# An eleven-block transformer step on one core: in masked attention two of four transposed score tiles get their mask by a ScalarE copy and a GpSimd addition

## The reference, cut to what matters

```
q, k, v = heads(x @ wq + bq), heads(x @ wk + bk), heads(x @ wv + bv)   # 16 heads of depth 16
scores = einsum('bhqd,bhkd->bhqk', q, k) / sqrt(16)
scores = scores + (1.0 - attention_mask * padding_mask) * -1e9          # only in the first attention
attn = softmax(scores); out = einsum('bhqk,bhkd->bhqd', attn, v) @ wo + bo
...
amax = max(abs(x2d), axis=-1); x_scale = maximum(amax, 1e-6) / 127.0
x_q = clip(round(x2d / x_scale), -128, 127)                             # 8-bit layer
```

## Time and profile before

| | before |
|---|---|
| median of 3 runs | 1608.37 us (1607.35 to 1613.48) |
| the profiled execution | 1603.58 us, its span 1601.8 us, mean granted clock 0.899 |
| PE busy in the span | 81% |
| DVE busy | 59% |
| ACT busy | 41% |
| POOL busy | 29% |

### The profile page before, as it was taken

One profiled execution on the slowest core, in us unless ns is written; L12 is line 12 of the kernel. 1 busy time (PEld: TensorE's weight loads), 2 busy tenths in 40 slices (PEclk: granted clock), 3 DMA queues, 4 the chain that ended last, 5 costly groups with the idle time before them and its releaser, 6 DMA issues. The chain is left out here.

```text
span 1601.8 us, 17931 instructions
## 1 busy us (share of the span) xinstructions
PE 1300.8 (81%) x5544; PEld 568.2 (35%) x5545; DVE 948.9 (59%) x2143; ACT 664.1 (41%) x1238; POOL 465.0 (29%) x608
## 2 busy tenths in 40 slices
PE   3588877878788989979969979988898669897970
PEld 1131232322323333523523523532323235564640
DVE  3699989899886655465465466457575132232323
ACT  1155545455455646355345345345555411021220
POOL 4260534422212322163163263234111006100016
PEclk9598989989899999979989979979999779998995
DMA  3833422313433521212212222223321088322214
GB/s 113 278 115 79 132 79 74 126 53 118 141 86 96 173 82 54 92 54 60 74 53 60 73 53 60 73 80 84 101 69 41 33 276 270 122 81 72 82 49 148
DMA packets 134343, 158.53 MB, mean 99 GB/s; under 512 B 15088, under 2 KB 111856, under 8 KB 134000
## 3 DMA queue, kind: packets, MB, share of 16 engines
q1 hardware_dynamic: 115568, 130.19, 26.5%
q10 hardware_dynamic: 15616, 18.88, 3.6%
q0 software_dynamic: 3072, 8.39, 1.6%
HBM read 93.87 MB, written 62.96 MB: 98 GB/s over the span
## 5 line engine op out<-in xcount | busy, mean ns | idle before, releaser
L1027 DVE TENSOR_REDUCE Mx<-bank 128x1 f32<-128x512 f32 x512 | 341.6, 686 | 299.4 <-PE bank L813 295.7
L727 ACT ACTIVATE prob<-bank 128x512 f32<-128x512 f32 x512 | 290.1, 594 | 272.8 <-PE bank L829 271.2
L813 PE MATMUL bank<-KS,QS 96*128 96x512 bf16 x768 | 318.9, 415 | 76.5 <-DVE Mx L1027 43.1
L829 PE MATMUL bank<-QS,KS 99*128 99x512 bf16 x768 | 314.2, 411 | 61.6 <-DVE prob L1038 28.3
L727 ACT ACTIVATE prob<-prob 128x512 f32<-128x512 f32 x256 | 161.0, 629 | 181.6 <-DVE prob L1038 180.0
L842 PE MATMUL bank<-prob,V 128*17 128x512 f32 x1536 | 231.3, 678 | 0.7 <-ACT prob L727 0.7
L813 PEld LDWEIGHTS bank<-KS,QS 96*128 96x128 bf16 x768 | 77.0, 100 | 303.1 <-DVE Mx L1027 116.0
L829 PEld LDWEIGHTS bank<-QS,KS 99*128 99x128 bf16 x768 | 76.4, 100 | 279.4 <-ACT prob L727 130.9
L561 POOL TENSOR_TENSOR rstd<-ve,minus_half 128x4 f32<-128x4 f32 x28 | 28.7, 1025 | 288.7 <-DVE ve L976 288.7
L581 POOL TENSOR_SCALAR MR<-neg 16x128 bf16<-16x128 f32 x48 | 13.8, 288 | 310.0 <-ACT neg L701 310.0
L1038 DVE TENSOR_TENSOR prob<-bank,ff_h 128x512 f32<-128x512 f32 x128 | 87.7, 685 | 17.6 <-PE bank L829 17.2
(11 more groups left out here) (151 smaller groups left out, 1742.1 us busy)
## 6 DMA issues: line engine op xcount, KB each, us to landing
stack_scr<-parts SPq DMA_DIRECT2D x48, 384.0 KB, 2.6
QS<-stack_scr SPq DMA_DIRECT2D x48, 384.0 KB, 4.0
KS<-stack_scr SPq DMA_DIRECT2D x48, 384.0 KB, 4.8
stack_scr<-parts SPq DMA_DIRECT2D x48, 256.0 KB, 2.9
w_gu<-in_gate_up ACTq DMA_DIRECT2D x16, 512.0 KB, 4.7
stack_scr<-parts SPq DMA_DIRECT2D x48, 128.0 KB, 2.7
disp<-zero SPq DMA_DIRECT2D x2, 3072.0 KB, 12.8
xr<-disp SPq DMA_DIRECT2D x48, 128.0 KB, 2.0
```

What stands on the lines that cost most here:

```text
L727: act.activation(prob[:, U % NP_, j, :], src, ACT.Exp, scale=CAST).then_inc(exp_done, 1)
L813: pe.matmul(bankS[i % NS][:, :], QS[0:STACK, v, qt * P:(qt + 1) * P], KS[0:STACK, v, :], start=True, stop=True).then_inc(s_full, 1)
L829: pe.matmul(bankT[e % NT][:, :], KS[0:ROWS, h, kt * P:(kt + 1) * P], QS[0:ROWS, h, :], start=True, stop=True).then_inc(t_full, 1)
L1027: dve.tensor_reduce(dst, b, AX.X, ALU.max).then_inc(s_read, 1)
```

## The change

1. In streams 0 to 3 the transposed tiles with j = 0 and 2 are no longer read by DVE: ACT copies the tile from PSUM to `prob` (`move`), POOL adds the mask in place (`plus_mask`), and ACT takes the exponential (`exponent`). Tiles with j = 1 and 3 stay as they were. The exponential of tile j = 2 stands in the next unit, after the copy of its tile 0; `values` moves from slot 2 to slot 3.
2. The preparation of a mask is an operation of its own, `fill`; it stands directly behind the transfer `mask` except for `fill(0, 1)`, which moves from step 2 to step 5, behind two cuts. `fill(0, 0)` is now DVE's.
3. Prologue: DVE takes the first statistics before its blank fills; the three rows of ones in `KS` come by a transfer in place of a DVE memset; ACT loads its table with a dummy exponential.
4. Layer norms: DVE's addition of epsilon is now POOL's. `affine` and `residual` work in halves of 128x512 in place of 128x1024.
5. Quantisation: the row scale (`xscale`) is worked out by POOL in place of DVE, the reciprocal stands a step later, POOL only does the first of three passes, DVE clamps, and ACT takes the offset away and writes bf16.

```diff
-            put(late, s - 1, ("mask", p, 0))
+            put(late, s - 1, ("mask", p, 0), ("fill", p, 0))
             put(late, s if p == 0 else max(s, first - 6), ("mask", p, 1))
+            put(late, 5 if p == 0 else max(s, first - 6), ("fill", p, 1))
...
-            put(early, e + 2, *halves("apply", p, a), ("affine", p, a))
-            put(late, e + 4, ("turn", p, a), ("res", p, a))
+            put(early, e + 2, *halves("apply", p, a), *halves("affine", p, a))
+            put(late, e + 4, ("turn", p, a), *halves("res", p, a))
...
+                            sp.dma_start(KS[STACK:ROWS, :, :].rearrange("r h (c q) -> r (h c) q", q=P),
+                                         ones_b[0:ROWS - STACK, :].unsqueeze(1)
+                                         .broadcast_to([ROWS - STACK, H * S // P, P])).then_inc(ones_in, 16)
...
+                def step_of(p):
+
+                    pool.wait_ge(amax_ready, p + 1)
+                    pool.tensor_scalar(xscale[p][:, :], amax[:, :], 1e-6, 1.0 / 127.0, ALU.max, ALU.mult)\
+                        .then_inc(xscale_ready, 1)
+
+                def plus_mask(n, u, j):
+
+                    U = n * UNITS + u
+                    if u < QT and j == 0:
+                        pool.wait_ge(mask_ready[1], QT * n + u + 1)
+                    pool.wait_ge(t_moved, moved(U, j))
+                    pool.tensor_tensor(prob[:, U % NP_, j, :], prob[:, U % NP_, j, :],
+                                       mb[n % 2][:, QT + u % QT, :], ALU.add).then_inc(t_added, 1)
...
+                    act.wait_ge(t_masked if j % 2 else t_added, moved(U, j))
+                    act.activation(dst, dst, ACT.Exp, scale=CAST).then_inc(exp_done, 1)
...
+                    if j == 1 and 0 <= u - 1 < (UNITS - 1 if n == B - 1 else UNITS):
+                        exponent(n, u - 1, 2)
                     if 0 <= u < UNITS:
...
+                        if j % 2 == 0:
+                            move(n, u, j)
+                        if j == 3:
+                            exponent(n, u, 0)
+                        if j % 2:
+                            exponent(n, u, j)
...
-                    link(dve.tensor_reduce(amax[:, :], T[p][:, :, :], AX.X, ALU.max, apply_absolute_value=True))
-                    link(dve.tensor_scalar(xscale[p][:, :], amax[:, :], 1e-6, 1.0 / 127.0, ALU.max, ALU.mult))
+                    dve.tensor_reduce(amax[:, :], T[p][:, :, :], AX.X, ALU.max, apply_absolute_value=True)\
+                        .then_inc(amax_ready, 1)
...
-                    if 0 <= u - 1 < UNITS and j == AV_AT:
+                    if 0 <= u - 1 < UNITS and j == (AV_AT if n >= B else HG - 1):
                         values(n, u - 1)
...
-                    if n < B and 0 <= u < UNITS:
+                    if n < B and 0 <= u < UNITS and j % 2:
                         masked(n, u, j)
```

More of the change, by code:

```diff
@@ L82, in batch_order @@
             put(early, s, *halves("apply", p, 0))
-            put(late, s, ("turn", p, 0), ("res", p, 0))
+            put(late, s, ("turn", p, 0), *halves("res", p, 0))
             for i, (m, what) in enumerate(((0, "k"), (0, "q"), (1, "k"), (1, "q"))):
@@ L122, in batch_order @@
                 put(early, e + 20, *halves("apply", p, 4))
-                put(late, e + 20, ("amax", p), ("res", p, 4))
-                put(early, e + 21, ("quant", p))
-                put(late, e + 22, ("i8T", p))
-                put(early, e + 23, ("i8turned", p))
+                put(late, e + 20, ("amax", p), *halves("res", p, 4))
+                put(early, e + 21, ("xrec", p))
+                put(late, e + 21, ("quant", p))
+                put(early, e + 22, ("clamp", p), ("round", p))
+                put(early, e + 23, ("i8T", p))
+                put(early, e + 24, ("i8turned", p))
                 put(late, e + 24, ("i8", p))
@@ L129, in batch_order @@
                 put(early, e + 26, *halves("apply", p, 5))
-                put(late, e + 26, ("turn", p, 5), ("res", p, 5))
+                put(late, e + 26, ("turn", p, 5), *halves("res", p, 5))
         for g in range(NG):
@@ L168, in batch_order, with moved @@
     return order
+def moved(U, j):
+    return 2 * U + j // 2 + 1
 def max_group(u):
@@ L628, in masks, with affine @@
                         link(pool.tensor_scalar(m, m, pm_col[p][:, kt:kt + 1], 1.0, ALU.mult, ALU.add))
-                        pool.tensor_scalar(m, m, NEG, 0.0, ALU.mult, ALU.add).then_inc(mask_ready[p], 1)
-                def affine(p, i):
+                        pool.tensor_scalar(m, m, NEG, 0.0, ALU.mult, ALU.add).then_inc(mask_ready[1], 1)
+                def affine(p, i, half):
                     if (p, i) == (0, 1):
@@ L667, in _ @@
                         quantise(*at)
-                    elif kind == "mask":
+                    elif kind == "fill" and at != [0, 0]:
                         masks(*at)
+                    elif kind == "amax":
+                        step_of(*at)
+                    elif kind == "tiles" and at[0] < B and 0 <= at[1] < UNITS and at[2] % 2 == 0:
+                        plus_mask(*at)
                     elif kind == "affine":
@@ L736, in _, with exponent @@
-                act.wait_ge(consts_dve, 2)
+                def exponent(n, u, j):
+                    U = n * UNITS + u
+                    e, dst = U * HG + j, prob[:, U % NP_, j, :]
+                    if n >= B:
+                        act.wait_ge(t_full, e + 1)
+                        act.activation(dst, bankT[e % NT][:, :], ACT.Exp, scale=CAST).then_inc(exp_done, 1)
+                        return
+                    act.wait_ge(t_masked if j % 2 else t_added, moved(U, j))
+                    act.activation(dst, dst, ACT.Exp, scale=CAST).then_inc(exp_done, 1)
@@ new lines, in move, with out_read @@
+                def move(n, u, j):
+                    U = n * UNITS + u
+                    e = U * HG + j
+                    act.wait_ge(t_full, e + 1)
+                    act.activation(prob[:, U % NP_, j, :], bankT[e % NT][:, :], ACT.Copy).then_inc(t_moved, 1)
+                def out_read(n, u):
+                    g = n * NG + u // QT - 1
+                    act.wait_ge(av_done, n * UNITS + u)
+                    if g >= 2:
+                        act.wait_ge(m_full, JOB[("oT", (g - 2) // NG, (g - 2) % NG)] + 1)
+                    act.activation(oT[:, g % 2, :], bankO[:, :], ACT.Copy).then_inc(o_read, 1)
@@ L737, in _ @@
+                act.wait_ge(consts_pool, 8)
+                act.activation(warm[:, :], ones_b[:, 0:1], ACT.Exp)
+                act.wait_ge(early_in, EARLY)
                 for kind, *at in ORDER:
@@ L745, in _ @@
                         normalise(*at)
+                    elif kind == "round":
+                        p = at[0]
+                        act.wait_ge(clamped, p + 1)
+                        act.activation(xq[p], T[p][:, :, :], ACT.Identity, bias=minus_magic[:, 0:1])\
+                            .then_inc(xq_ready, 1)
                     elif kind in ("turn", "attT"):
@@ L1081, in _ @@
                         statistics(*at)
+                        if at == [0, 0, 1]:
+                            blanks()
+                            dve.wait_ge(early_in, EARLY)
+                    elif kind == "fill" and at == [0, 0]:
+                        first_mask()
+                    elif kind == "xrec":
+                        shares(*at)
+                    elif kind == "clamp":
+                        clamp(*at)
                     elif kind == "apply":
```

172 lines of the change are left out of this document (100 added, 72 removed).

## The result

The changed kernel takes 1636.04 us (median of 4 runs, 1634.73 to 1639.88) beside 1608.56 us of the kernel before on the same chip: a ratio of 1.0169, 95% interval 1.0141 to 1.0196. It is slower by 1.7%; forecast were 1555 us.

The account below looks back on a forecast made before the run. DVE was taken to bound the masked streams (90% busy) and PE those without mask. Prologue 20.7, masked streams 20 (60 less 40) and quantisation 12 off 1603.6 gave 1550.9, put at 1555 us as the execution was 4.8 under median; range 1515 to 1590.

Parts of the forecast that it names:

- Part 1: Prologue: earlier statistics and POOL's split no longer delayed bring the first score tile at 32.7 us, a gain of 20.7 us.
- Part 2: Masked streams: moving 128 of DVE's 256 additions to ACT copies and POOL additions gains 60 us, before mask preparation losses.
- the ceiling is 77 us: Masked streams: most that removing 128 DVE additions at 0.60 us each could gain, checked against stream 4's 77.5 us.
- Part 3: Masked streams: mask preparations on POOL now stand ahead of its tile additions and lose 40 us of the 60.
- the three second masks: Preparations of batches 1 to 3's second masks on POOL delay additions: 5.5, 3 and 3 us lost.
- The first masks: Preparations of batches 1 to 3's first masks on POOL delay tiles: 8, 10 and 10 us lost.
- The others run on for a while: While POOL's addition is late, PE goes on until slot 2 of the next unit, about 3.5 us.
- Part 4: Quantisation: DVE's scale operation, held by POOL's additions up to 4.11 us, moves to POOL; 12 us gained.
- (A): Rival: queues are elastic and the mask preparations cost nothing, 1515 us; chance 0.16 (below 1530).
- (B): Rival: other POOL work between additions also costs; masked streams gain nothing or lose up to 25, 1575 to 1600; chance 0.15.
- (C): Rival: POOL's additions and DVE hold each other up in the masked streams, 1661 us; chance 0.07 including any other loss.
- or another loss: Any loss of the whole kernel by a cause not listed; no size given, shares the chance 0.07 with (C).

Follow-up runs that it names:

- e15_dve_finer: e9_finer with all four transposed tiles of a group masked by DVE as in the kernel before; 1583.01 us, 0.9827 of the kernel before.
- e9_finer: e2_spread with the two halves of each residual and scale-and-shift put a step apart in all layers; 1557.48 us, 0.9693 of the kernel before.
- e3_dve_tiles: Changed kernel with all four transposed tiles masked by DVE again and `values` in slot 2; 1598.67 us, 0.9805 of the kernel before.
- e8_no_tmask: e3_dve_tiles without DVE's mask additions on transposed tiles, exponentials reading PSUM; 1520.43 us, 0.9450 of the kernel before.
- e4_nofill: Changed kernel with earlier mask transfers and the mask preparations of batches 1 to 3 left out; 1600.14 us, 0.9805 of the kernel before.
- e2_spread: Changed kernel with earlier mask transfers and each preparation of batches 1 to 3 spread over four steps; 1597.70 us, 0.9791 of the kernel before.
- e0_after: The changed kernel measured again without edit, on the chip of some follow-up runs; 1660.86 us, 1.0201 of the kernel before.
- e11_scale_dve: Changed kernel with the quantisation's 128x4 scale operation moved back from POOL to DVE; 1640.52 us, 1.0202 of the kernel before.

## Why the prediction was wrong

**Part 1 was right**, 32.1 us for 32.7. The first mask's preparation on DVE ended in time, though it met POOL's residual in the prologue:

```profile
14.52 3.19 POOL L691 TENSOR_TENSOR R<-R,b_row 128x512 f32<-128x512 f32 x2 [5.90 <-DMA b_row<-in_brow]
```

```profile
14.15 0.43 DVE L1091 TENSOR_SCALAR mask<-mask 128x512 f32<-128x512 f32 x1
...
15.21 1.37 DVE L1091 TENSOR_SCALAR mask<-mask 128x512 f32<-128x512 f32 x1
```

The same DVE operation took 0.43 us and then 1.37 beside the residual. By the Trainium skill, "SBUF — State Buffer", section "SBUF: two separate sides", the one of the two engines that starts first has the shared ports for its whole instruction when DVE is in a two-port mode, or reads two inputs from SBUF beside a GpSimd operation that reads it. The trace agrees: this operation took 0.94 us longer, the next one, with two inputs, 1.75 us where the one before had taken 0.69, and POOL's pair 3.19 us where such a pair takes 2.48 at 74.20 us.

**Part 2 failed**, in the step "the ceiling is 77 us ... I take 60 of the 77, by estimate, so 0.94 us of a plain unit's 4.8", that is, 0.94 us in each of 64 units. Measured: 5.5 us with spread preparations (382.3 to 376.8), 14.4 with finer pieces (382.3 to 367.9; 18.5 against e15_dve_finer), 11.7 with POOL's additions out. In e9_finer the 16 units 9 to 12 did give 12.3 us against e3_dve_tiles, 0.77 each; the other 48 gave 2.1 together. The ceiling priced every one of DVE's additions at 0.60 us, from a plain unit, and checked it against the 77 us of stream 4; e8_no_tmask, without any of them, takes 76.7 us in stream 0 but 80.7 to 87.1 in streams 1 to 3, where the layer work of two batches sets the length of some units. All 256 are worth 52.7 us, so 128 could not bring 77. Against the half that is given away stand the copies, 8 to 10 us, and POOL's lateness, 10 to 12 against e4_nofill and 6 to 8 against e2_spread. PE's waits show what came in DVE's place. In the masked streams of e3_dve_tiles PE waited 64.3 us for DVE and 1.7 for ACT and POOL, in e9_finer 31.7 and 31.4. The largest of both (e3_dve_tiles first):

```profile
PE bank L908 <- DVE prob L1136: 26.7, 92, 1.2
PE bank L888 <- DVE Mx L1122: 22.6, 78, 0.9
```

```profile
PE bank L907 <- DVE Mx L1143: 13.4, 43, 0.8
PE bank L929 <- DVE prob L1157: 13.1, 35, 1.2
PE bank L929 <- ACT prob L787: 11.2, 17, 3.4
PE bank L942 <- ACT oT L796: 7.5, 12, 0.8
PE bank L868 <- POOL R L687: 5.9, 3, 2.1
PE bank L868 <- ACT R L766: 5.4, 2, 2.9
```

Half of the waiting for DVE has gone and as much waiting for ACT's copies and results and for layer norm rows (`R`) of ACT and POOL has come. The forecast had taken 17 us off its ceiling for such coupling. Why the first half of the additions brings so much less than the second is not settled beyond that; DVE's remaining additions stand in slots 1 and 3 with a maximum behind each, and no run evened them out.

**Part 3 had the mechanism and was too small**: 40 us taken, 64.0 measured as the difference of e0_after and e2_spread (4.6 before the first values product, 59.4 behind it), of which 39.5 are POOL waiting and 24.5 POOL computing. The terms that were mis-sized are the three second masks, 5.5 us for batch 1 and "I take 3 each" for batches 2 and 3: the two units around each (3 and 4 of streams 0, 1 and 2) were 14.0, 13.9 and 16.1 us longer than the same units before, as in the changed order additions stand right behind the preparation, and the output projection does not cover it. The first masks were near the forecast: 4.6 us ahead of the first values product where 8 were taken, and units 13 to 15 of streams 0 and 1 longer by 11.2 and 11.8 us where 10 each were. "The others run on for a while" gave back 2.6 us in that place and not 3.5: PE stood 9.25 us for an addition that came 11.9 us after the one before it had ended (110.99 less 99.11). And the half clock after each stop was not in the sum: PE's busy time for the same 1343 to 1346 records is 315.7 us in e0_after and 305.5 in e2_spread, 10 of the 59, beside granted clocks of 0.87 and 0.92.

**Part 4 had the size; its cause is at most a part.** -9.8 us where -12 was forecast, and no operation of 4 us. PE's waits for row maxima in streams 4 to 10 fell from 38.6 to 19.3 us, where the forecast had three waits of over 4 us in mind. But the held operation put back cost nothing, and with its collision mostly taken out of the kernel before streams 6 to 9 were 5.6 us shorter, of 13.7 that the change gains there, and the whole kernel no faster (1606.20 beside 1606.35 us). In e9_finer and e15_dve_finer, with pieces of POOL's work a step apart, streams 6 to 9 take another 7.7 and 3.7 us less (451.5 and 455.5), which speaks for the halves and their order as the rest; the change's own halves were not tried alone, so it stays open. So it is in part luck that the size came out nearly right.

**The rivals.** (A) did not come. (B) came by its mechanism, splits, residuals and the like between additions, but worth 6 to 12 us, and only with the preparations did the streams lose 50. (C) not: DVE's additions took 684 and 685 ns beside POOL's 1271 (685 before), its maxima 700 and 698 (690 before). A loss had 0.07 with (C) "or another loss", and none of the rivals had this one: it is part 3 by its own step, 24 us larger, over a part 2 that gave 5.5 us in the masked streams in place of 60.

## What to carry to other kernels

A busy engine's time in a plain unit is not what an operation is worth in all units: leave the operation out once, for all units, and read the ceiling there, before sharing its work out. Then look which waits the sharing puts in the place of those that it takes. When work on the critical path moves to an engine that has been a quiet helper, everything in that engine's queue becomes critical, the waits for transfers first: issue the transfers earlier and cut long pieces so that one stands in each step. Here that turned 1.017 to 1.020 into 0.969; the same orders with all tiles left on DVE come to 0.983.

## What was not expected of the hardware

TensorE's granted clock was 0.97 in the 10 us in which it began to starve and 0.50 in the 8 us of work behind its wait of 9.25 us, so here a hold-up cost more than its length; over the masked streams it was 0.87 against 0.92 to 0.96 in the versions without such hold-ups. A DVE operation of 0.17 us was held for over 3 us in three batches of e11_scale_dve without any effect on streams 6 to 9 (459.1 us with and without). PE had a values product and feed-forward work just then; whether that is the reason was not tested.
